# Batch 1's shared expert: one of four input groups multiplied as whole numbers and scaled per output channel, with the first norms reordered

## The reference, cut to what matters

```python
x = x + _layernorm(_L0_attn_ref(_layernorm(x), ...))      # state-space scan
x = x + _layernorm(_L0_ffn_ref(_layernorm(x), ...))       # this step
x = x + _layernorm(_L1_attn_ref(_layernorm(x), ...))      # attention inside a token
x = x + _layernorm(_L1_ffn_ref(_layernorm(x), ...))       # mixture step

# _L0_ffn_ref: HIDDEN 512, INTER 1376, GROUPSIZE 128, 4-bit weights
# dequant: w[k,n] = q[k,n]*s[g,n] - (z[g,n]+1)*s[g,n],  g = k // 128
gate = x2 @ Wg
up = x2 @ Wu
inter = gate * jax.nn.sigmoid(gate) * up
out = (inter @ Wd).astype(jnp.float16)
```

## Time and profile before

| | |
|---|---|
| median of 3 runs | 805.58 us (805.26 to 806.01) |
| the profiled execution | 807.46 us, of which its span is 805.6 us |
| busy over the span: PE, DVE, ACT, POOL | 683.4, 688.1, 469.8, 480.6 us |
| the expert, batch 1, blocks 1 to 10 | about 581.4 to 669.6 us of the span |

### The profile page before, as it was taken

The page is one execution under the profiler, slowest core; times in us unless marked ns, Lnnn a source line. Parts: engine busy times, 40 slices in busy tenths (PEclk is TensorE's granted clock), DMA queues, the critical chain, the costliest instruction groups (busy, mean ns, idle before and its releaser), DMA issues. The chain is left out here.

```text
span 805.6 us, 8451 instructions
## 1 busy us (share of the span) xinstructions
PE 683.4 (85%) x2794; PEld 325.1 (40%) x2794; DVE 688.1 (85%) x701; ACT 469.8 (58%) x805; POOL 480.6 (60%) x252
## 2 busy tenths in 40 slices
PE   7979899988687788564637889999999999999995
PEld 6623333323122222111112224444445556887885
DVE  6889999999999999999999998998274576485778
ACT  5478778895656774867664447756325347323333
POOL 2429999999999999999999960220002014331130
PEclk9999979999888997858867989999999999999998
DMA  8434232335503714731235309971040030000011
GB/s 262 92 101 142 75 129 71 119 130 180 186 4 120 246 37 158 229 131 36 96 131 179 102 12 259 256 221 55 1 157 1 1 105 0 1 1 1 0 53 52
DMA packets 42326, 83.19 MB, mean 103 GB/s; under 512 B 6809, under 2 KB 10308, under 8 KB 42028
## 3 DMA queue, kind: packets, MB, share of 16 engines
q1 hardware_dynamic: 42284, 82.66, 32.4%
HBM read 71.43 MB, written 11.21 MB: 103 GB/s over the span
## 5 line engine op out<-in xcount | busy, mean ns | idle before, releaser
L2388 POOL TENSOR_TENSOR dbu<-rep_du,bc 128x1024 f32<-128x1024 f32 x127 | 296.5, 2359 | 1.8 <-ACT rep_du L2054 0.9
L1880 ACT ACTIVATE psum<-rep_dt,aneg 128x512 f32<-128x512 f32 x256 | 166.2, 682 | 117.4 <-DVE hc L1230 96.1
L1219 DVE TENSOR_TENSOR_SCAN psum<-psum,dbu 128x1024 f32<-128x1024 f32 x89 | 203.4, 2285 | 3.4 <-ACT psum L1880 1.5
L970 PE MATMUL psum<-hc,stk 128*32 128x512 f32 x512 | 84.4, 736 | 62.1 <-POOL hc L2397 44.3
L1230 DVE TENSOR_TENSOR hc<-psum,bc 128x1024 f32<-128x1024 f32 x89 | 109.0, 1224 | 3.1
L2397 POOL TENSOR_TENSOR hc<-hc,bc 128x1024 f32<-128x1024 f32 x39 | 91.8, 2355 | 7.7 <-DVE hc L1219 7.7
L1219 DVE TENSOR_TENSOR_SCAN hc<-psum,dbu 128x1024 f32<-128x1024 f32 x39 | 89.0, 2281 | 1.0 <-ACT psum L1880 0.9
L709 PE MATMUL psum<-xf_hi,gu_hi 128*128 128x512 f16 x176 | 66.8, 379 | 0.4 <-ACT sg L2181 0.4
L709 PE MATMUL psum<-xf_hi,gu_lo 128*128 128x512 f16 x176 | 66.8, 379 | 0.0
L709 PE MATMUL psum<-xf_lo,gu_hi 128*128 128x512 f16 x176 | 66.8, 379 | 0.0
L709 PE MATMUL psum<-xT,w_g 128*128 128x512 f32 x120 | 58.7, 636 | 2.6 <-ACT rep_du L2025 2.6
(11 more groups left out here) (305 smaller groups left out, 1453.0 us busy)
## 6 DMA issues: line engine op xcount, KB each, us to landing
rep_dt<-rep_scratch SPq DMA_DIRECT2D x60, 256.0 KB, 3.3
rep_du<-rep_scratch SPq DMA_DIRECT2D x60, 256.0 KB, 4.1
cw<-c_scratch SPq DMA_DIRECT2D x11, 768.0 KB, 12.0
qw<-qgu_in SPq DMA_DIRECT2D x11, 512.0 KB, 6.8
bc<-bc_scratch SPq DMA_DIRECT2D x16, 256.0 KB, 5.0
rep_scratch<-du_t SPq DMA_DIRECT2D x14, 256.0 KB, 2.0
rep_scratch<-dt_t SPq DMA_DIRECT2D x14, 256.0 KB, 2.3
qw<-qd_in SPq DMA_DIRECT2D x11, 256.0 KB, 8.1
```

The source lines that it names most:

```text
L970: last = pe.matmul(y_rows(k), stk[:], hc[:, (i + k // 2) % HCS, k % 2, :], start=False, stop=(s == GN - 1))
L1219: dve.tensor_tensor_scan(h, a, dbu[:, i % DBS].rearrange("p e t -> p (e t)"), 0.0, ALU.mult, ALU.add)\
L1880: last = act.activation(psum[:, 2 * (i % 2) + e, :], rep_dt[:, cc % 2, k, :], ACT.Exp, scale=aneg[:, k, c, n:n + 1])
L2388: pool.tensor_tensor(dbu[:, i % DBS], rep_du[:, cc % 2, k:k + 2, :], bc[:, n, :].unsqueeze(1).broadcast_to([P, 2, L]), ALU.mult).then_inc( ...
```

## The change

In batch 1, for the blocks 1 to 10, the last group of 128 inputs is taken out of the g and u products. Its weights are the whole numbers q - z - 1, which float16 holds exactly, so two matmuls do (whole x xf_hi, whole x xf_lo) instead of three. They go to Y_BANK; ACT copies the bank with a scale per output channel into sg (for g) or `it` (for u); DVE adds the nine-matmul product from the ring bank to that, once for g (`gate_sum`) and once for u (`up_sum`). Silu then reads sg in SBUF, and `times_sum` multiplies the two. There is one Y_BANK: the pair for u waits until ACT has scaled that of g, and the pair for the next g until ACT has scaled that of u.

SP keeps the whole numbers of each block with a copy out of `cw` within SBUF (64 KB each, `keep_ints`), before the slot is loaded again, and loads the 2816 scales of that group in two DMAs of single float16 numbers.

The order also changes: the sums over wqraw and bqraw go ahead of batch 1's loop on DVE; the first tile's norm and addition (`ffn_inv16`, `ffn_add16(0, 0)`) go between `up_sum(1)` and `times_sum(1)`, and the others move up by one; `gate_sum(6)`, `(7)` and `(8)` stand inside the attention's steps; on ACT `root(("moe", 0))` goes ahead of block 9's scaling.

```diff
+            def keep_ints(i):
+                sp_.wait_ge(q16_used, i + 1)
+                sp_.dma_start(ints[i][:], cw[i % SLOTS][:, 0, 2 * (KH - 1) * P:2 * KH * P]).then_inc(ints_kept, 16)
             def stage_again(i):
+                if i > SLOTS:
+                    sp_.wait_ge(ints_kept, 16 * (i - SLOTS))
                 sp_.wait_ge(wlo_gu, i - SLOTS + 1)
...
             stage(3)
+            keep_ints(1)
             for i in range(SLOTS, IC):
                 stage_again(i)
+                if i > SLOTS:
+                    keep_ints(i - SLOTS + 1)
+            sp_.wait_ge(ints_kept, 16 * (IC - SLOTS))
+            keep_ints(IC - 3)
...
+            keep_ints(IC - 2)
+            keep_ints(IC - 1)
+            for j in range(2):
+                sp_.dma_start(group16[:, j, :], sgu_in[...].rearrange("r (i n) -> n (r i)", n=P), ...)
...
+                def group_part(i, j):
+                    if i > 1 or j:
+                        pe.wait_ge(group_done, 2 * (i - 1) + j)
+                    else:
+                        pe.wait_ge(ints_kept, 16 * (IC - 1))
+                    w = ints[i][:, j * P:(j + 1) * P]
+                    pe.matmul(psum[:, Y_BANK, :], w, xf_hi[1][:, KH - 1, :], start=True, stop=False)
+                    pe.matmul(psum[:, Y_BANK, :], w, xf_lo[1][:, KH - 1, :], start=False, stop=True)\
+                        .then_inc(group_ready, 1)
...
-                        for kk in range(KH):
+                        for kk in range(KH - 1 if grouped else KH):
...
+                        if grouped:
+                            group_part(i, j)
                         product(item, parts).then_inc(work_ready, 1)
...
+            def gate_sum(i):       # DVE: sg = bank + sg, waits for the product and group_done 2i-1
+            def up_sum(i):         # DVE: it = bank + it, waits for the product and group_done 2i
+            def times_sum(i):      # DVE: it = sg * it, waits for silu_done i
...
+            dve.wait_ge(ld_att, 16 * 7)
+            dve.tensor_reduce(wqkv[:, :, 0:DH], wqraw[:], AX.X, ALU.add).then_inc(wq_done, 1)
+            dve.tensor_reduce(bqkv[:, 0:DH], bqraw[:], AX.X, ALU.add).then_inc(wq_done, 1)
+            dve.wait_ge(ld_group, 32)
+            dve.tensor_copy(group32[:], group16[:]).then_inc(group_set, 1)
             for i in range(IC):
+                if i and i not in (6, 7, 8):
+                    gate_sum(i)
                 if i == IC - 1:
                     low_moe(0, [2, 3])
-                ffn_times(1, i)
+                if i:
+                    up_sum(i)
+                    if i == 1:
+                        ffn_inv16(0)
+                        ffn_add16(0, 0)
+                    times_sum(i)
+                else:
+                    ffn_times(1, i)
...
                 if i == 7:
+                    gate_sum(8)
                     between(0, 8)
...
+            def group_scaled(i, j):
+                k = IC + i
+                if i == 1:
+                    act.wait_ge(group_set, 1)
+                act.wait_ge(group_ready, 2 * (i - 1) + j + 1)
+                if j:
+                    act.wait_ge(itlo_done, k - 1)
+                act.activation((it if j else sg)[:, k % 2, :], psum[:, Y_BANK, :], ACT.Identity,
+                               scale=group32[:, j, i:i + 1]).then_inc(group_done, 1)
+            def ffn_silu_sum(i):
+                k = IC + i
+                wait_taken(act, ("g", 1, i))
+                act.activation(sg[:, k % 2, :], sg[:, k % 2, :], ACT.Silu).then_inc(silu_done, 1)
...
-                ffn_silu(k)
+                if b == 1 and i >= 1:
+                    if i - 1 not in (0, 2, 5, 6, 8):
+                        group_scaled(i, 0)
+                        group_scaled(i, 1)
+                    ffn_silu_sum(i)
+                else:
+                    ffn_silu(k)
...
                 if b == 1:
+                    if i in (2, 5, 6, 8):
+                        act.preload_act_table_set(LOG_EXP)
+                    if i == 8:
+                        root(("moe", 0), NT)
+                    if i in (0, 2, 5, 6, 8):
+                        group_scaled(i + 1, 0)
+                        group_scaled(i + 1, 1)
```

More of the change, by code:

```diff
@@ L300, in build @@
         cs = [at(f"cs{s}", STG[s] + 12, [SZ], F16) for s in range(AHEAD)]
+        ints = {i: at(f"ints{i}", 35 + (i - 1) / 2 if i < 9 else {9: 21.25, 10: 24}[i], [2 * P], F16)
+                for i in range(1, IC)}
+        group16 = at("group16", 206.625, [2, IC], F16)
+        group32 = at("group32", 206.75, [2, IC])
         q16 = [at("q16_0", 149, [SZ], F16), at("q16_1", 203, [SZ], F16)]
@@ L449, in build @@
         it_done = sem("it_done")
+        silu_done = sem("silu_done")
+        ints_kept = sem("ints_kept")
+        group_set = sem("group_set")
+        group_ready = sem("group_ready")
+        group_done = sem("group_done")
+        ld_group = sem("ld_group")
         ithi_done = sem("ithi_done")
@@ L670, in _ @@
             load(bet[:], beta_in.broadcast_to([P, H]), ld_att)
+            keep_ints(IC - 2)
+            keep_ints(IC - 1)
+            for j in range(2):
+                sp_.dma_start(group16[:, j, :], sgu_in[2 * (KH - 1) + j:2 * KH - 1 + j, :]
+                              .rearrange("r (i n) -> n (r i)", n=P),
+                              allow_slow_non_contiguous=True).then_inc(ld_group, 16)
             sp_.wait_ge(wq_done, 2)
@@ L673, in _ @@
             load(moe_w["wr"][0][:], wr_dram.rearrange("(k p) n -> p k n", p=P), ld_moe[0])
+            sp_.wait_ge(ints_kept, 16 * (IC - 1))
             sp_.wait_ge(wlo_gu, IC)
@@ L999, in down @@
                     last.then_inc(ffn_used, 1)
+                def group_part(i, j):
[7 more added lines that the diff above has]
+                        .then_inc(group_ready, 1)
                 for i in range(IC):
                     k = b * IC + i
+                    grouped = b == 1 and i >= 1
                     if b == 0:
@@ L1441, in ffn_times @@
                     .then_inc(taken_sem(("u", b, i)), 1)
+            def gate_sum(i):
+                k = IC + i
+                item = ("g", 1, i)
+                wait_work(dve, item)
+                dve.wait_ge(group_done, 2 * i - 1)
+                dve.tensor_tensor(sg[:, k % 2, :], bank(item), sg[:, k % 2, :], ALU.add).then_inc(taken_sem(item), 1)
+            def up_sum(i):
+                k = IC + i
+                item = ("u", 1, i)
+                wait_work(dve, item)
+                dve.wait_ge(group_done, 2 * i)
+                dve.tensor_tensor(it[:, k % 2, :], bank(item), it[:, k % 2, :], ALU.add).then_inc(taken_sem(item), 1)
+            def times_sum(i):
+                k = IC + i
+                dve.wait_ge(silu_done, i)
+                wait_taken(dve, ("u", 1, i))
+                dve.tensor_tensor(it[:, k % 2, :], sg[:, k % 2, :], it[:, k % 2, :], ALU.mult).then_inc(it_done, 1)
             def ffn_low(b, i):
@@ L1489, in att_scores @@
                 link(dve.tensor_reduce(smax[:], sc[:], AX.X, ALU.max))
+                if b == 0:
+                    gate_sum(6)
                 dve.tensor_tensor(sc[:], sc[:], smax[:].unsqueeze(3).broadcast_to(full), ALU.subtract)\
@@ L1498, in att_values @@
                 dve.tensor_reduce(num[:], sc[:], AX.X, ALU.add)
+                if b == 0:
+                    gate_sum(7)
                 link(dve.reciprocal(den[:], den[:]))
@@ L1520, in between @@
                 if i == 1:
-                    ffn_inv16(b)
-                    ffn_add16(b, 0)
-                    ffn_add16(b, 1)
+                    if b == 0:
+                        ffn_add16(b, 1)
+                        ffn_add16(b, 2)
+                    else:
+                        ffn_inv16(b)
+                        ffn_add16(b, 0)
+                        ffn_add16(b, 1)
                 if i == 2:
-                    ffn_add16(b, 2)
+                    if b:
+                        ffn_add16(b, 2)
                     ffn_add16(b, 3)
@@ L1600, in _ @@
                 ffn_low(1, i)
[L1601 to L1604, removed]
                 if i < 8:
@@ L2181, in ffn_silu @@
                 act.activation(sg[:, k % 2, :], bank(item), ACT.Silu).then_inc(taken_sem(item), 1)
+            def group_scaled(i, j):
+                k = IC + i
+                if i == 1:
[6 more added lines that the diff above has]
+            def ffn_silu_sum(i):
+                k = IC + i
+                wait_taken(act, ("g", 1, i))
+                act.activation(sg[:, k % 2, :], sg[:, k % 2, :], ACT.Silu).then_inc(silu_done, 1)
             def ffn_high(k):
                 b, i = divmod(k, IC)
-                wait_taken(act, ("u", b, i))
+                if b == 1 and i >= 1:
+                    act.wait_ge(it_done, i)
+                else:
+                    wait_taken(act, ("u", b, i))
                 if k >= 2:
@@ L2263, in _ @@
                 if b == 1:
+                    if i in (2, 5, 6, 8):
```

(5 more changed lines are left out.)

## The result

The changed kernel takes 814.04 us (median of 4 runs, 813.13 to 815.4) against 805.8 for the kernel before on the same chip: ratio 1.0093, 95% interval 1.0073 to 1.0112. It is slower by 0.9%, clear of the scatter. Its profiled execution took 815.4 us with a span of 813.5, 7.9 us more than the span before.

A forecast was written before the change was run, and what follows sets the result against it. PE was taken to bound batch 1's blocks. Gaps of 11.8 us less 4.7 saved gave +7.1, SP +0.3: 805.6 + 7.1 + 0.3 = 813.0 us, range 809 to 817 (the forecast's own 810.5 to 815).

The forecast's parts named there:

- The bound and the new wait: Batch 1's blocks: PE bounds; block i-1's tail, wanted at T + 5.18 us, is now wanted before T + 2.38.
- The breaks: PE's gaps before u's pair in blocks 1 to 10 and at the last down(10), 11.8 us in sum, 4.3 in block 9.
- The scaled copy: ACT's 20 copies of a bank from PSUM with one operand per channel, taken as 0.69 us each.
- The saving: PE in batch 1's blocks: 20 matmuls fewer, 4.3 us, plus the break at 592 gone, 0.4; together 4.7 us.
- Blocks at full clock: Batch 1's blocks: gaps of 11.8 us less 4.7 saved, +7.1 us.
- SP: Batch 0's stages: stage(6) issued only at about 509.7, stage(8) 0.1 to 0.3 us late; taken as +0.3 us.
- One sign that the prediction gave against itself: Batch 0: DVE waiting for `cw` or `qw` by more than 0.5 us would show the SP reckoning wrong.
- The table load: ACT's table load takes 1.28 us without a drain; by the skill's 2.66 the time would be some 4 us longer.
- The gain: Second rival: block tails do not stand in the way, only small gaps stay, 801 to 802 us; chance 0.10.
- Half of the breaks: Fourth rival: chains in the blocks coupled less tightly, so half of the gaps, 807 us; chance 0.08.
- The SP rival: Third rival: each copy holds SP for 2 us, stages land later, 3 to 4 us left, 816.5 us; chance 0.08.
- The clock rival: First rival: as forecast, but PE's clock falls in block 9's gap, price 1.7 us, 814.7 us; chance 0.14.

The follow-up runs named there:

- eleven matmuls alone: Kernel before, with eleven matmuls instead of twelve for g and for u in batch 1's blocks 1 to 10, part of the computation missing: 805.26 us, ratio 0.998.
- SP's part alone: Kernel before plus only SP's whole-number copies, the stages' waits for them and the unread single-number loads: 805.37 us, ratio 0.9981.

## Why the prediction was right, point by point

**The bound and the new wait.** Right. PE is on the path, and the tail of a block, free up to `down` before, now stands ahead of u's pair. Taking 3.44 us out of the tail took 3.45 from PE's wait; moving the copy past it took the wait away.

**The breaks.** Forecast was how late the pair is, which is the loss:

| block | 1 | 2 | 3 | 4 | 5 | 6 | 7 | 8 | 9 | 10 | down(10) | sum |
|---|---|---|---|---|---|---|---|---|---|---|---|---|
| forecast | 0.05 | 0.7 | 0.4 | 1.3 | 0.1 | 0 | 1.7 | 1.6 | 4.3 | 0.1 | 1.5 | 11.8 |
| loss | 0 | 0.68 | 0.51 | 1.25 | 0 | 0 | 1.76 | 1.60 | 4.29 | 0 | 1.55 | 11.6 |

Carrying each engine's own list forward with durations of the trace was worth the work: every break was in its place and within about 0.1 us. `ffn_low(7)` came at 645.87 (forecast 645.7), PE got block 9's copy at 658.14 (658.0).

**The scaled copy.** Taken as 0.69 between 0.591 and 0.779; measured 0.67 to 0.69.

**The saving.** 4.7 us counted, 5.0 measured. The old breaks were taken as 0.4 and were 0.68: the one at 592 was read from its bracket (0.16 too small), and with the 0.14 of the other they are 0.54 and not 0.4. The run with eleven matmuls alone showed how easily this term could have failed: without the moved sums 2.7 of 4.3 us would have been lost to tails of the old kernel. The prediction named the move as the reason why `gate_sum(1)` is in time, but gave it no price; in the kernel with eleven matmuls it was 2.2 us (91.17 - 88.93). It also read the chain in these blocks as one row of PE after the other, which it is only from 592 on: from 581.6 to 592.3 the chain lies on DVE and ACT, the two sums in it.

**Blocks at full clock.** Forecast +7.1, measured 99.6 - 92.8 = +6.8.

**SP.** Forecast +0.3; no cost measured in SP's part alone, and 0.16 at `unpack(6)` in the changed kernel, too little to tell from none. The mechanism was there, since `stage(6)` did wait for its copy, but the step was put at 509.7 and came at 507.01. One sign that the prediction gave against itself is there too: at 490.57 DVE waited 0.93 us for `cw`, where the kernel before has two such waits, 0.34 and 0.20. It reached the blocks as no more than these 0.16.

**The clock.** Here the prediction chose the wrong case. It gave the fall in block 9's break a chance of 0.14 and a price of 1.7 us; it came in each of three profiles with that break, at 2.4, 2.9 and 1.5 us. The step that failed set the certainty of a 4 us stop against batch 0's qkv, where PE had narrow work to do and no stop. By the Trainium skill (TensorE: Matmul & The Clock Gate, part 1) half rate is the default and activity releases it, so that the fall was the likelier case; these traces agree, with three falls in three stops of 4.1 us and none where matmuls filled the stop.

That the time was still about 1 us from the forecast (814.04 against 813.0) is partly luck. In the profiled pair the clock's +2.4 in the blocks was nearly made up by the 1.6 that the profile of before had lost at batch 1's qkv, by the 0.3 of SP and by the 0.3 of the old breaks; how often either fall came in the runs behind the medians is not known. Of the twelve profiled runs three fell at that place (before, the one without the attention's addition, the one with the old order of the norms), so I hold it for chance and not for an effect of the change; the runs do not prove that.

**The table load.** 1.28 us, and the roots began 0.02 later (655.59, 656.89): no drain, as read from the earlier trace rows. The 2.66 us of the Trainium skill (ScalarE: Activation LUTs, section What ACT_TABLE_LOAD costs) would, by an estimate from it, have made block 9's loss 5.7 us; it was 4.29.

**The rivals.** The gain fell: the wait is there. Half of the breaks fell: the sum is 11.6. The SP rival fell. The clock rival was right as to its mechanism.

## What to carry to other kernels

Before matmuls are traded for work on other engines, look not only at their idle share but at where in their lists the piece stands that PE will wait for, and at what stood there with slack. Here 13.8 + 13.8 us of added work were less than the idle time, and the blocks still grew, because a hand-over bank put a 12 us tail ahead of u's products, and the added sums stand in that tail too. If such a hand-over is needed, put its release ahead of the tail: 5.0 us of blocks for one moved instruction, 2.4 of them clock. That is not the whole cost: with the release moved in all six blocks they still took 96.0 us at full clock against 92.8 before. Of the versions that group blocks, only the one with three, which leaves the attention's blocks alone, had shorter blocks than before. A second hand-over bank was not tried. And test the saving alone: a bound engine that becomes faster meets the next tail, and 4.3 us were worth 1.6 until the two sums in that tail were moved too.

## What the runs showed of the hardware

- TensorE's clock fell to its lower level in a stop of 4.1 us in all three profiled executions that had one, and stayed there for 6.8, 6.8 and 3.4 us, at a cost of 2.4, 2.9 and 1.5 us; 17 matmuls in the stop kept it at 1.00 (one profile). Stops of 1.1 to 1.6 us in the same blocks did not lower it, nor did one of 2.6 us (one profile).
- At the narrow qkv matmuls (3.5 us, 48 columns) the clock fell behind in some executions and not in others: at batch 0's in one of twelve profiles, at batch 1's in three. It then stayed at 0.50 for 3.4 us.
- A bracketed idle time of PE understates what a break costs by 0.16 us for matmuls of 512 columns, since the end of a matmul is modelled 0.38 us after its start and the pace is 0.216.
- Ten 64 KB copies within SBUF, most of them queued behind 1.5 MB of loads, took 6.2 us to land (median; one took 8.9) and held back the issue of the loads that waited for them by 7.5 us at `stage(6)`, without DVE being late. Two DMAs of 1408 single numbers of 2 bytes each took 3.3 and 3.7 us to land, where I had guessed 11 for both.
